# The last pass of a convolution, attention and expert kernel: who adds the first experts' rows to the residual

## What is computed

```python
    t = t + _L1_attn_ref(_ln_t(t), ...)
    t = t + _L1_ffn_ref(_ln_t(t), L1_ffn_Wg, L1_ffn_W1, L1_ffn_W2)

    def _L1_ffn_ref(x, Wg, W1, W2):
        router_logits = jnp.einsum('bsd,de->bse', x, Wg)
        top_logits, top_idx = jax.lax.top_k(router_logits, TOP_K)      # TOP_K = 2
        top_w = jax.nn.softmax(top_logits, axis=-1)
        combine = jnp.sum(jax.nn.one_hot(top_idx, E, dtype=x.dtype) * top_w[..., None], axis=-2)
        ...
        for e in range(E):
            h = jax.nn.silu(xt @ W1[e]) @ W2[e]
            out = out + cw[:, e:e + 1] * h
```

## Time and profile before

| | us |
|---|---|
| median of 3 timed runs | 744.64 |
| lowest and highest of them | 744.32, 746.57 |
| the profiled execution, its own time | 735.71 |
| its span, first to last instruction | 733.8 |
| last pass: SyncE's first load to the end of the span | 713.68 to 733.8 |

### The profile page before, as it was taken

One profiled execution on the slowest core, in us unless ns is written; L12 is line 12 of the kernel. 1 busy time (PEld: TensorE's weight loads), 2 busy tenths in 40 slices (PEclk: granted clock), 3 DMA queues, 4 the chain that ended last, 5 costly groups with the idle time before them and its releaser, 6 DMA issues. The chain is left out here.

```text
span 733.8 us, 11191 instructions
## 1 busy us (share of the span) xinstructions
PE 598.2 (82%) x3561; PEld 515.9 (70%) x3561; DVE 473.5 (65%) x1216; ACT 310.6 (42%) x615; POOL 261.9 (36%) x292
## 2 busy tenths in 40 slices
PE   5699999838788999979799797876309999999920
PEld 4488888626578998879789787876207888888810
DVE  5675784755557678757768576775315777777725
ACT  3221222233345353534425244434008888888800
POOL 3041454567000101131413114142740666666660
PEclk9899999958989999999989899999558999999975
DMA  8999445520431404050321305000149777777109
GB/s 260 381 358 359 148 161 173 172 101 0 144 116 30 144 1 144 2 173 1 116 58 66 110 1 170 4 30 12 48 141 298 221 241 234 243 240 245 59 10 334
DMA packets 56375, 105.47 MB, mean 144 GB/s; under 512 B 8872, under 2 KB 21817, under 8 KB 56192
## 3 DMA queue, kind: packets, MB, share of 16 engines
q1 hardware_dynamic: 51328, 96.24, 40.1%
q0 software_dynamic: 4992, 8.54, 3.3%
HBM read 58.15 MB, written 48.42 MB: 145 GB/s over the span
## 5 line engine op out<-in xcount | busy, mean ns | idle before, releaser
L1481 PE MATMUL bank<-rvx,s_expd 128*128 128x96 f32 x1024 | 135.3, 278 | 12.6 <-ACT s_expd L995 6.9
L1481 PEld LDWEIGHTS bank<-rvx,s_expd 128*128 128x128 f32 x1024 | 128.5, 197 | 15.8 <-ACT s_expd L995 8.7
L995 ACT ACTIVATE s_expd<-bank 128x512 f32<-128x512 f32 x128 | 75.6, 598 | 120.1 <-PE bank L1465 98.4
L1157 DVE TENSOR_REDUCE s_max<-bank 128x2 f32<-128x512 f32 x128 | 87.2, 689 | 56.7 <-PE bank L1444 40.8
L1744 POOL DMA_INDIRECT y_slots<-virt,pad_l x92 | 95.2, 1035 | 72.3 <-issue 44.7
L883 POOL TENSOR_TENSOR ln_rstd<-ln_var,power 128x4 f32<-128x4 f32 x16 | 16.4, 1024 | 200.9 <-DVE ln_var L1133 200.8
L914 POOL DMA_INDIRECT x_slots<-rows,slot_of x64 | 62.9, 983 | 68.0 <-DVE rows L1284 44.1
L1783 DVE TENSOR_TENSOR k_stack<-virt,k_stack 128x512 fp32r<-128x512 f32 x92 | 63.5, 690 | 24.5 <-ACT k_stack L1763 20.4
L53 PE MATMUL bank<-pad_h,u_h 128*128 128x512 f32 x144 | 60.7, 422 | 14.4 <-DVE pad_l L395 8.1
L1465 PE MATMUL bank<-q_stack,k_stack 100*128 100x256 f32 x256 | 60.8, 320 | 5.3 <-DVE q_stack L1175 5.3
L1763 ACT ACTIVATE k_stack<-virt 128x512 fp32r<-128x512 f32 x92 | 58.1, 632 | 9.1 <-PE bank L55 1.8
(11 more groups left out here) (251 smaller groups left out, 1246.2 us busy)
## 6 DMA issues: line engine op xcount, KB each, us to landing
x_slots<-blank SPq DMA_DIRECT2D x8, 2112.0 KB, 20.2
pad_h<-w_split SPq DMA_DIRECT2D x23, 512.0 KB
q_stack<-w_split SPq DMA_DIRECT2D x23, 512.0 KB
qk_rows<-qk SPq DMA_DIRECT2D x16, 512.0 KB
k_stack<-qk_rows SPq DMA_DIRECT2D x96, 64.0 KB, 2.2
q_stack<-qk_rows SPq DMA_DIRECT2D x48, 128.0 KB, 2.4
pad_l<-x_slots SPq DMA_DIRECT2D x23, 264.0 KB
e_raw<-in_w SPq DMA_DIRECT2D x16, 256.0 KB, 3.0
```

Source lines behind the costliest of these rows:

```text
L995: nc.scalar.activation(expd[:, s % 2].rearrange("p a i -> p (a i)"), ps_st[s % 2][:, :], ACT.Exp).then_inc(exp_done, 1)
L1157: nc.vector.tensor_reduce(s_max[:, :, s], ps_s[s % 2][:, :].rearrange("p (a j) -> p a j", a=2), AX.X, ALU.max).then_inc(max_done, 1)
L1481: last = pe.matmul(ps_pv[s // 4][:, at:at + RVW], expd[:, s % 2, a, i * P:(i + 1) * P], rvx[:, ring, 2 * b + a, :], start=(a == 0), stop=( ...
```

## The change

In the last pass GpSimd takes over half of the loads. After its last scatter it waits for both `y_placed` itself and issues four DMAs that read the first experts' rows from `y_slots` and add them to `sums` as they are moved (`accum_op=ALU.add`). Each covers two chunks, so 4096 bytes of each partition, 512 KB in all. SyncE issues only the eight loads of the second experts' rows. VectorE's eight `add_first` are gone; `add_other` of chunk n waits for its own load and for the GpSimd transfer that covers the chunk. For that the four transfers count up semaphores that have served their turn elsewhere: the two `y_placed`, and the two `scattered` of the attention stage (`first_in`). The tile region `y_first` and the semaphore `first_added` are no longer used.

```diff
-    y_first = f32(k_stack[:, 0])
...
+    first_in = [(y_placed[0], 16 * G * ((NB + 1) // 2) + 16), (y_placed[1], 16 * G * (NB // 2) + 16)
+                ] + [(half, 2 * G * 16 * (NCH // 2) + 16) for half in scattered]
...
+    def all_placed(eng):
+        eng.wait_ge(y_placed[0], 16 * G * ((NB + 1) // 2))
+        eng.wait_ge(y_placed[1], 16 * G * (NB // 2))
+
+    def token_rows(k):
+        return y_slots[k * TOK:(k + 1) * TOK].rearrange("(p n j) f -> p n (j f)", p=P, n=NCH)
...
-        sp.wait_ge(y_placed[0], 16 * G * ((NB + 1) // 2))
-        sp.wait_ge(y_placed[1], 16 * G * (NB // 2))
+        all_placed(sp)
         for n in range(NCH):
-            for k, dst in enumerate((y_first, y_other)):
-                src = y_slots[k * TOK:(k + 1) * TOK].rearrange("(p n j) f -> p n (j f)", p=P, n=NCH)
-                sp.dma_start(dst[:, n], src[:, n]).then_inc(rows_in[n], 16)
+            sp.dma_start(y_other[:, n], token_rows(1)[:, n]).then_inc(rows_in[n], 16)
...
+        all_placed(pool)
+        for m in range(NCH // 2):
+            two = slice(2 * m, 2 * m + 2)
+            pool.dma_start(sums[:, two], token_rows(0)[:, two], accum_op=ALU.add).then_inc(first_in[m][0], 16)
...
-        def add_first(n):
-            dve.wait_ge(rows_in[n], 16 * tiles_on(n) + 32)
-            nc.vector.tensor_tensor(sums[:, n], sums[:, n], y_first[:, n], ALU.add).then_inc(first_added, 1)
-
         def add_other(n):
-            dve.wait_ge(first_added, n + 1)
+            dve.wait_ge(rows_in[n], 16 * tiles_on(n) + 16)
+            dve.wait_ge(*first_in[n // 2])
             nc.vector.tensor_tensor(sums[:, n], sums[:, n], y_other[:, n], ALU.add).then_inc(summed, 1)
...
         for n in range(NCH):
-            add_first(n)
-            if n:
-                add_other(n - 1)
-        add_other(NCH - 1)
+            add_other(n)
```

More of the change, by code:

```diff
@@ L1670, in experts @@
     y_placed = [sem("y_placed0"), sem("y_placed1")]
-    first_added = sem("first_added")
     summed = sem("sums_ready")
```

## The result

The changed kernel takes 750.96 us (median of 4 runs, 748.21 to 754.68) against 744.48 us before (median of 4, 740.97 to 746.57). The ratio is 1.0135, with a 95% interval of 1.0086 to 1.0183: slower. The medians lie 6.5 us apart; the ratio stands for 10 us, with 6 to 14 us as the ends of its interval. The forecast was 750.6 us. The profiled execution took 748.21 us, with a span of 746.1 us.

A forecast was written before the change was run, and what follows sets the result against it. The prediction took the nearly full stream of DMA transfers to bound the last pass. Its six terms, all 0 but the second read's +6.0 us, added to the 744.64 us median gave 750.6 us, range 743.0 to 757.5 us.

The forecast's parts named there:

- Part 1: Last pass: eight additions leave VectorE, 5.5 us of busy time, worth 0 on the path while the transfer stream is full.
- Part 2: Last pass: eight loads leave SyncE's queue, freeing it from about 718 us, but no sum is ready to store: worth 0.
- Part 3: Last pass: GpSimd issues four transfers at 1.3 us each, 5.4 us, done near 719 us; cost 0.
- Part 4: Last pass: adding transfers also read the old `resid`, 2.1 MB more for the DMA engines: +6.0 us, between 5.2 and 7.3.
- Part 5: Early stretch of the last pass: a second queue could fill holes in the DMA stream, gaining 0 to 2.0 us; taken as 0.
- Part 6: End of the last pass: a hole of up to 2.5 us if adding transfers finish last; taken as 0.
- The hidden read: Rival, last pass: the old value is read alongside, adding costs like a plain transfer, 744.6 to 747 us; chance 0.19.
- the shorter stream: Rival, last pass: hidden read and two queues keep engines full, 15.6 us in place of 18.0, 742.2 us; chance 0.08.
- The slow adder: Rival, last pass: adding takes longer than fetching or waits for both reads, +12.0 us, 756.6 us; chance 0.17.
- What was said to stay: Before the last pass: the waits for the last scatters, the last scatter and SyncE's first load stay where they are.

The follow-up runs named there:

- the three pairs: The changed kernel, as it is, timed three times beside the kernel before: ratios 1.0135, 1.0193 and 1.0105.

## Why the prediction was right

*What bounds the last pass.* The stream of transfers does, as read from the table of stretches. Taking the eight additions away gained nothing (20.0 against 19.8 us), and making the stream longer by 5.6 us of engine time made the pass 5.0 to 6.1 us longer.

*Part 1*, the additions, at 0: borne out by the kernel that leaves the first additions out (20.0 against 19.8 us). *Part 2*, SyncE's issues, at 0: borne out by the two kernels that take eight plain loads off its queue. The pass is 20.2 us with GpSimd's queue and 19.6 us with ScalarE's.

*Part 3*, GpSimd's issues at 1.3 us each, cost 0: the cost was right and the size wrong on the safe side. All four took 3.66 us, 0.9 us each.

*Part 4*, the second read, +6.0 us with 5.2 and 7.3 us as its ends: borne out. The last pass grew by 5.0, 6.1 and 4.9 us in the three profiles (25.2, 26.3 and 25.1 against 20.2 us with plain transfers), and the engines' time on that queue by 5.6 us. The rate that fits the engines' time lies between the two that the prediction weighed, 404 GB/s (5.2 us) and the mean of 348 (6.0 us). What is shown is the price, that of one more read of the 2.1 MB. That it is a read, and not an adder that takes as long as one, is argued and not shown: no run adds without a second read. This agrees with the second of the two sentences that the prediction took from "Collectives: The Full Stack" in the Trainium skill, the two source reads at half the rate: 2.04 times the engines' time here. The first, that the addition is free, may hold for the adding itself, but the transfer as a whole is not free.

*Part 5*, two queues fill the holes, 0: right. On one chip the early stretch ran at 310 GB/s with one queue and at 322 with ScalarE's beside it, and the pass was at most 0.2 us shorter. With GpSimd's plain transfers it ran at 307 in the first 5 us.

*Part 6*, the hole at the end, 0: right. The adding transfers were done by about 738 us, and SyncE's loads landed last (the waits for `pad_h<-y_slots` at 736.28 and 739.50 us). What was left of loads and stores kept the engines full, at 395 GB/s. The reason given, larger rows and so a larger share, fits the kernel with eight transfers of smaller rows, where the adding ones finished last.

*The rivals.* The hidden read would have left the pass at 20.1 us, the shorter stream at 18; both fell. The slow adder would have made it 31 us or more, and fell in that size.

*What was said to stay.* The last scatter was to stand where it was, and in the profiles it did not: 718.84, 717.98 and 720.75 us against 711.54 and 713.16 us on chips of a like total. The sum had nothing for the time ahead of the last pass, and what of it is the change's stays open.

*The total.* The median came out 0.4 us from the forecast, and that closeness is luck. The last pass accounts for 5.0 to 6.2 us, the ratio stands for 10 us with 3.6 us either way, and over the three pairs the medians differed by 6.5, 8.2 and 4.4 us. The direction and the range held, and so did the mechanism in the last pass.

## What to carry to other kernels

Read the DMA share of a stretch beside the compute timeline before moving work from an engine to a transfer. Where the DMA engines were full, an addition made while moving wasn't free: it took twice the engines' time of a plain load. Whether it pays where they idle was tried once, in the scatters of the expert loop, and there GpSimd's longer issue and the later landing cost far more than the saved pass.

To compare variants that differ in one stage, read the length of that stage from each profile. Here it repeated within 0.4 us for the kernel before, over totals that lay 30 us apart, and within 1.2 us for the changed one. And profile the kernel before on every chip that is used. The early stretch of the same kernel ran at 286 GB/s on one and at 310 on another, which is more than the second queue changed, and the long tiles stay unexplained for want of such a profile.

## What the runs showed of the hardware

- A transfer that adds 4096 or 2048 bytes a partition onto the on-chip residual took 5.1 to 5.6 us of the 16 DMA engines for each MB, against 2.6 us for a plain load on the same queue. The bytes reported are no more than those of the plain load, so that the engines can be full (1.04) at 231 GB/s.
- Adding scatters of 512-byte rows to HBM took 9.9 us a MB against 2.6 us, in packets about five times smaller, and each kept GpSimd 1.55 us against about 1.0 us for its 128 rows. It landed 4.2 us after its issue in the median.
- GpSimd hands over direct transfers faster than scatters: four adding ones in 3.66 us, where a scatter follows another every 1.3 us. Of eight in a row the eighth was held back, and issued only at 732.96 us after 3.20 us of idle time.
- The same kernel takes 714.8 us on one chip and 737.5 to 744.5 us on three others, while its last pass is the same on all that were profiled.
